# Three phases over edge tiles made into one software-pipelined loop, with the softmax state of a source node in one table

## The reference

```
# layer 3 (equivariant), after the per-edge messages were summed by node into agg
s_in, v_in = agg[..., 0:2], agg[..., 2:8]            # 64 channels, scalar and 3-vector
os1 = softplus(s_in @ w_f2o1_s / 8) - log 2 ; ov1 = v_in @ w_f2o1_v / 8
x3  = layernorm(x2 + concat(os1 @ w_f2o2_s, ov1 @ w_f2o2_v) / sqrt(128))
# layer 4 (attention over edges, 8 heads of 64, grouped by source node)
q, k, v = split(x3 @ W) ; aw = sum(q[src] * k[dst]) / 8    # one score per edge and head
e = exp(aw - segment_max(aw, src)[src])
out[n] = sum over edges of n (e * v[dst]) / sum(e)
x4 = layernorm(x3 + out)
```

## Time and profile before

| | us |
|---|---|
| three runs | 2404.39, 2409.9, 2411.34; median 2409.9 |
| the profiled execution's own time | 2407.08 |
| its span, first to last instruction | 2405.4 |

### The profile page before, as it was taken

How to read it: one execution, slowest core, us unless ns; L and a number is a source line. 1 busy time by engine, 2 the same in 40 slices (tenths; PEclk the granted TensorE clock), 3 DMA queues, 4 the chain that set the end, 5 groups by cost and what they waited for, 6 DMA issues and landing times. The chain is left out here.

```text
span 2405.4 us, 24073 instructions
## 1 busy us (share of the span) xinstructions
PE 1907.2 (79%) x5516; PEld 938.7 (39%) x5516; DVE 1583.2 (66%) x2672; ACT 1038.4 (43%) x1968; POOL 1007.9 (42%) x1095
## 2 busy tenths in 40 slices
PE   5999995999999999999999790055487699967800
PEld 2444442444444444444444340033255444423300
DVE  5464552577777777777776060799568679867854
ACT  2353442455555555555554230244278623313332
POOL 2211112466665666666656532456322012224334
PEclk9999998999999999999999895555568799979855
DMA  7632113444444444444443633433333222227743
GB/s 259 244 130 58 18 22 56 164 158 151 153 158 144 159 155 146 163 147 156 157 142 136 199 64 48 114 84 88 101 126 123 104 90 106 106 79 193 211 136 110
DMA packets 159454, 310.19 MB, mean 129 GB/s; under 512 B 31890, under 2 KB 45107, under 8 KB 159127
## 3 DMA queue, kind: packets, MB, share of 16 engines
q1 hardware_dynamic: 126278, 233.65, 28.0%
q0 software_dynamic: 29760, 71.21, 13.1%
q10 hardware_dynamic: 3344, 4.51, 0.6%
HBM read 169.54 MB, written 139.76 MB: 129 GB/s over the span
## 5 line engine op out<-in xcount | busy, mean ns | idle before, releaser
L659 PE MATMUL d_p_h<-w3a,d_xT 128*128 128x512 f32 x640 | 290.5, 597 | 25.4 <-DMA d_xT<-in_xT 25.4
L659 PE MATMUL d_p_o<-d_w,d_uT 128*128 128x512 f32 x640 | 289.9, 596 | 3.0 <-ACT d_uT L734 3.0
L659 PE MATMUL d_p_p<-d_wr,d_x1T 128*128 128x512 f32 x640 | 289.0, 595 | 0.0
L550 POOL TENSOR_SCALAR d_small<-d_mv 128x1 f32<-128x1 f32 x160 | 81.9, 512 | 303.5 <-DVE d_mv L785 153.7
L816 DVE TENSOR_TENSOR d_zz<-d_yg,d_xbeta 128x512 f32<-128x512 f32 x80 | 138.5, 1731 | 98.9 <-POOL d_yg L867 98.9
L659 PEld LDWEIGHTS d_p_h<-w3a,d_xT 128*128 128x128 f32 x640 | 122.8, 192 | 180.4 <-issue 180.4
L659 PEld LDWEIGHTS d_p_o<-d_w,d_uT 128*128 128x128 f32 x640 | 122.1, 191 | 156.6 <-issue 152.0
L727 ACT ACTIVATE d_yn<-d_y,d_small 128x512 f32<-128x512 f32 x80 | 65.1, 813 | 230.6 <-POOL d_small L555 230.6
L659 PEld LDWEIGHTS d_p_p<-d_wr,d_x1T 128*128 128x128 f32 x640 | 116.1, 191 | 115.9 <-issue 115.9
L282 PE MATMUL m_p_H<-m_xT,m_w 128*128 128x512 f32 x320 | 147.3, 615 | 4.8 <-ACT m_xT L323 4.8
L755 ACT ACTIVATE d_x<-d_zz,d_small 128x512 f32<-128x512 f32 x80 | 65.1, 814 | 178.4 <-POOL d_small L555 178.4
(11 more groups left out here) (252 smaller groups left out, 4239.2 us busy)
## 6 DMA issues: line engine op xcount, KB each, us to landing
sum<-d_zeros SPq DMA_DIRECT2D x80, 260.0 KB, 2.1
sum<-m_tile_sum SPq DMA_DIRECT2D x10, 2048.0 KB, 7.8
d_xT<-in_xT SPq DMA_DIRECT2D x80, 256.0 KB, 2.7
d_z<-sum SPq DMA_DIRECT2D x80, 256.0 KB, 2.9
d_x<-in_x SPq DMA_DIRECT2D x80, 256.0 KB, 3.4
x<-d_x SPq DMA_DIRECT2D x80, 256.0 KB, 2.0
p<-d_p SPq DMA_DIRECT2D x80, 256.0 KB, 2.0
pair_p<-p SPq DMA_DIRECT2D x40, 512.0 KB, 3.8
```

Source lines behind the costliest of these rows:

```text
L550: nc.gpsimd.tensor_scalar(tmp, var, factor, add, ALU.mult, ALU.add).then_inc(done, 1)
L659: last = nc.tensor.matmul(out[:, :], lhsT[:, c, :], w[:, c, :], start=(c == 0), stop=(c == KB - 1))
```

## The change

`equivariant_phase` and `scores_phase` become empty, and `values_phase` holds one block (names `f_`) with `STEPS = 25` steps. In step i, tile a = i is in the first product, b = i-1 in the second product and normalisation, c = i-2 in the queries and keys, d = i-3 in scores, tile maximum, values and weighing, e = i-4 in the merge with the node's state.

- The maximum is a running one. A new DRAM table `state` has 528 columns a node: for each head 64 weighted sums and the sum of weights, and at the end 8 maxima. For each tile POOL gathers the nodes' old state, DVE and ACT make the new maximum and the two factors exp(old max - new max) and exp(tile max - new max), DVE computes old * factor + tile sums * factor, and POOL scatters the result back (a plain write). `sum3`, `max3`, their gathers and the accumulating scatter are gone. The gather for tile t+1 waits until the scatter of t has landed.
- Scores are spread to all partitions by two transfers in place of PE and DVE work: SP writes the tile's 128x8 scores to DRAM, waits, and reads the row back broadcast to 128 partitions (512 KB). `cand` reads it with a stride of 8 elements.
- x3: the node's row is added by PE (identity times row, a 128x512 product) into the one `p_R`, whose vector part is written with a stride of 3 elements; ACT copies it out. DVE's two additions are gone, and w2s, w2v are scaled once.
- One buffer where there were two for `p_O`, `p_R`, `q`, `away` and `both`; queries and values share the PSUM bank `p_qv`. `outT` has 2 buffers of 2 units, where there were 3 of 4.
- Weights `wqk` (2 MB) and `wv` (1 MB) are loaded at the start, behind the first two pairs. Pairs are spread 3, 2, 2 and then 1, 2, 1, 2, ... over the 25 steps.
- `dense_phase` fills two tables in place of three; `attended_rows_phase` reads 528 columns and takes two reciprocals of 128x8 in place of one of 128x16.

The diff, cut to its core:

```diff
+def plain_plan(steps):
+    plan = [3, 2, 2] + [1 + i % 2 for i in range(steps - 3)]
...
-                sp.dma_start(rows(k.sum2, i), zeros[:, 0:8 * F]).then_inc(tables_set, 16)
-                sp.dma_start(rows(k.sum3, i), zeros[:, :]).then_inc(tables_set, 16)
-                sp.dma_start(rows(k.max3, i), lowest[:, :]).then_inc(tables_set, 16)
+                sp.dma_start(rows(k.sum2, i), empty[:, 0:8 * F]).then_inc(tables_set, 16)
+                sp.dma_start(rows(k.state, i), empty[:, :]).then_inc(tables_set, 16)
...
+        @block.sync
+            pair_load(nc, k, sp, 0)
+            pair_load(nc, k, sp, 1)
+            sp.dma_start(k.wqk, ...).then_inc(k.wqk_in, 16)
+            sp.dma_start(k.wv[:, :, :], ...).then_inc(k.wqk_in, 16)
+            for step in range(STEPS):
+                t = step - 3
+                if 0 <= t < T:
+                    sp.wait_ge(aw_done, t + 1)
+                    sp.dma_start(k.aw_rows[t, :]..., k.scores[:, t, :]).then_inc(aw_out, 16)
+                    sp.wait_ge(aw_out, 16 * (t + 1))
+                    if t:
+                        sp.wait_ge(cand_done, t)
+                    sp.dma_start(spread..., k.aw_rows[t:t + 1, :].to_broadcast([P, P * HEADS])).then_inc(spread_in, 16)
+                for _ in range(HERE[step - 1] if step else 0):
+                    if pair + 2 < PAIRS:
+                        pair_load(nc, k, sp, pair + 2)
+                    pair_store(nc, k, sp, pair)
+                    pair += 1
...
+        @block.gpsimd
+            for step in range(STEPS):
+                for u in (2 * step + AHEAD, 2 * step + AHEAD + 1):
+                    if u < 2 * T:
+                        gather_sums(u)        # waits until PE has turned unit u - 6
+                t = step - 4
+                if 0 <= t < T:
+                    scatter_state(t)          # waits for merged
+                    if t + 1 < T:
+                        gather_state(t + 1)   # waits until the scatter has landed
...
+        @block.tensor
+            for step in range(STEPS):         # (the "if tile in range" tests are cut)
+                second(b, 0)                  # waits ssp_done(b), y_done of the unit before
+                turn_x3(c, 0); turn_x3(c, 1)
+                second(b, 1)
+                turn_sums(a, 0)
+                queries(c)
+                first(a, 0); turn_sums(a, 1)
+                values(d)
+                first(a, 1)
+                keys(c)
+                tile_sums(d)                  # waits vw_done(d)
...
+        @block.scalar
+            for step in range(STEPS):
+                second_product_out(b, 0)      # y_done
+                x3_turned_out(c, 0); x3_turned_out(c, 1)
+                second_product_out(b, 1)
+                sums_turned_out(a, 0)
+                state_factors(e); away_from(d); query_out(c)
+                first_product_out(a, 0); sums_turned_out(a, 1)
+                x3_rows(b)
+                weights(d)                    # waits less_done(d)
+                first_product_out(a, 1); logarithms(a)
+                for _ in range(HERE[step]):
+                    pair_normalise(nc, k, act, pair)
+                    pair += 1
...
+        @block.vector
+            for step in range(STEPS):
+                scores(d); new_maximum(e)     # the latter waits old_in(e)
+                moments(b, 0); moments(b, 1)  # wait y_done
+                merge(e)                      # three 128x520 instructions
+                extra = HERE[step]
+                if extra:
+                    pair_leaky(nc, k, dve, pair)
+                    if extra == 1:
+                        pair_moments(nc, k, dve, pair)
+                        pair += 1
+                tile_maximum(d)               # cand, reduce, subtract: less_done
+                if extra > 1:
+                    pair_moments(nc, k, dve, pair)
+                    pair += 1
+                weigh_values(d)
+                softplus(a)                   # waits logarithms(a)
+                for _ in range(extra - 1):
+                    pair_leaky(nc, k, dve, pair)
+                    pair_moments(nc, k, dve, pair)
+                    pair += 1
```

More of the change, by code:

```diff
@@ new lines, in values_phase @@
+        cand = k.filters[:, :, :, :].rearrange("p t c f -> p (t c f)")[:, KB * 2 * D:KB * 2 * D + HEADS * P].rearrange(
+            "p (h e) -> p h e", h=HEADS)
+        away = sb("away", [P, P])
+        less, both = sb("less", [P, HEADS]), sb("both", [P, HEADS, HD + 1])
+        old = [sb(f"old{i}", [P, STATE + HEADS]) for i in range(2)]
+        new, part = sb("new", [P, STATE]), sb("part", [P, HEADS, HD + 1])
+        fall, factor = sb("fall", [P, 2, HEADS]), sb("factor", [P, 2, HEADS])
+        p_T = [ps(f"p_T{i}", [P, D]) for i in range(2)]
@@ new lines, in values_phase @@
+        q_done, q_out, k_done, prod_done, aw_done, aw_out, spread_in, away_done, cand_done, top_done, less_done = (
+            sem(n) for n in ("q_done", "q_out", "k_done", "prod", "aw", "aw_out", "spread_in", "away", "cand", "top",
+                             "less"))
+        weighed, v_done, vw_done, s_done, old_in, new_top, fall_done, factors, scaled, part_done, merged, gone = (
+            sem(n) for n in ("weighed", "v_done", "vw", "s_done", "old_in", "new_top", "fall", "factors", "scaled",
+                             "part", "merged", "gone"))
@@ L1444, in second @@
[L1444 to L1453, removed]
@@ new lines, in product, with queries @@
+            def product(out, xT, w, done):
+                for c in range(KB):
+                    last = nc.tensor.matmul(out[:, :], xT[:, c, :], w[:, c, :], start=(c == 0), stop=(c == KB - 1))
+                last.then_inc(done, 1)
+            def queries(t):
+                pe.wait_ge(turned_out, turn_number(t + 2, 0) + 1)
+                if t:
+                    pe.wait_ge(vw_done, t - 1)
+                    pe.wait_ge(q_out, t)
+                product(p_qv, srcT, k.wqk[:, :, 0:D], q_done)
@@ new lines, in weights, with state_factors @@
+            def weights(t):
+                act.wait_ge(less_done, t + 1)
+                if t:
+                    act.wait_ge(s_done, t)
+                nc.scalar.activation(both[:, :, HD], less[:, :], ACT.Exp).then_inc(weighed, 1)
+            def state_factors(t):
+                act.wait_ge(fall_done, t + 1)
+                if t:
+                    act.wait_ge(part_done, t)
+                nc.scalar.activation(factor[:, :, :], fall[:, :, :], ACT.Exp).then_inc(factors, 1)
+            nc.scalar.preload_act_table_set(ACT_SET)
@@ L1897, in _ @@
                 b, c = g % 2, g % BUFS
+                heads = [sums[c][:, s, 0:ATT].rearrange("p (h f) -> p h f", h=HEADS) for s in range(2)]
                 dve.wait_ge(sums_in[c], 32 * (g // BUFS + 1))
```

679 lines of the change are left out of this document (301 added, 378 removed).

## The result

The changed kernel is slower. Its median is 2433.4 us (2423.1 to 2434.6, five runs), that of the kernel before on the same chip 2404.4; the ratio is 1.0102, with a 95% interval of 1.0076 to 1.0129. The profiled execution's own time is 2433.4 us, 26 us above the 2407.1 of before.

What follows compares the result with a forecast made beforehand. DVE and PE, each 78% busy, were not full, so stream order decides. Steps end at 2303, the o phase starts at 2315 against 2313: +2, plus 10 of unseen costs, on 2407.1 gives 2419, forecast 2420; range 2375 to 2470.

Steps and rivals of the forecast that it cites:

- the side that had the higher chance: Whole kernel: slower, above 2417 us, was given 0.51, against 0.31 for faster and 0.18 for the same.
- DVE's work does not shrink: Fused loop: additions and diagonal go, the merge comes; 461 us of DVE work against 457 now.
- The two steps: Full loop: a two-pair step of 25.5 us and a one-pair step of 22.6, together 48.1 with 39.4 of DVE work.
- The stride at a tenth: Strided reads of cand and writes of p_R: a tenth more on cand, nothing on PE, 0.1 us a step.
- The third rival: Strided accesses at twice the price: cand 1.24 us more, PE's passes 0.7, in each of 20 steps; +39, 2458; 8%.
- Loads and state: Late pair loads behind the spread, 0.7 us in two steps, and late state scatter and gather, 0.4.
- The start: Steps 0 to 3: DVE starts at 1734, third pair lands at 1757, wanted at 1748; step 0 ends at 1764.
- The end: Steps from 20 on: 88.6 us in all, then 12 us from the last pair to the o phase's first gather.
- The first rival: Idle time in two steps falls from 8.7 to 4.4 us: -43 us, 2377; sign DVE over 88% busy; 27%.
- The second rival: Late normalisation holds y and state or pair transfers are late, at new_maximum or leaky: +32 us, 2450; 8%.
- The fourth: PE stays at the low clock: 34 us a step, +115 us, 2520; sign a clock under 0.7; 4%.

Runs made afterwards that it cites:

- kernels 3: The changed kernel with the stride of 8 elements moved from the addition of the candidates to the reduction that reads its result: 2433.2 us, ratio 1.0123.
- 12: The changed kernel with the spread table read contiguously, leaving out the reordering by head (maximum over the wrong scores): 2411.2 us, ratio 1.0038.
- kernel 5: The changed kernel with DVE adding the node rows itself again, without the identity product, ACT's copy and PE's stride: 2405.1 us, ratio 1.0002.
- kernel 1: The changed kernel with ACT normalising a step's last pair in the next step, behind the copies of y: 2410.5 us, ratio 1.0034.
- kernel 10: 7 plus the second half's product in the keys' PSUM bank and the logarithms ahead of the weights on ACT: 2373.6 us, ratio 0.9875.
- 13: kernel 10 with one maximum a node over all heads, so that the spread table is read contiguously: 2358.0 us, ratio 0.9809.
- kernel 11: 7 plus logarithms ahead of the weights on ACT and DVE adding the node rows itself: 2383.8 us, ratio 0.9916.
- 7: kernel 1 plus SP issuing a step's pair loads ahead of its wait for the scores: 2379.4 us, ratio 0.9891.

## Why the prediction held, and where not

Forecast 2420, measured 2433, in the range and on the side that had the higher chance. Against the kernel before it looks less good: +12 us were forecast and +26 measured on the profiled executions (+10 and +29 by medians), so the sign and the mechanism were right and the size was under half. On the own time of the profiled executions it was 2419 against 2433.4, 14 us short. By its terms:

- *DVE's work does not shrink*: right. 460.7 us busy for 461 forecast, though this hides an error: added up as I had added them, the durations are 477 us, 16 more, and the stride is 16. The busy time is lower because neighbouring records overlap a little. The merge, three times 0.70, and the softplus, 0.71, are as forecast.
- *The two steps*: the mechanism was right, each wait at its place. One-pair step: forecast waits 1.3 and 3.2, measured 1.51 and 3.62, and for the weights and logarithms some 2 forecast, 1.4 measured. Two-pair step: 0.7 and 1.5, measured 1.14 and 1.86, or 2.75 and 1.86 where PE began slowly. Per two steps the waits are 10.3 us (82.1 us in steps 4 to 19, in eighths) for 8.7 forecast, and all else 40.7 for 39.4. The means are 27.4 and 23.6 us for 25.5 and 22.6. The missing term is PE's clock after short stops: I gave the low level to the one stop of over 6 us, but four of the eight two-pair steps began slowly too, at 1.6 us each.
- *The stride at a tenth*: the step that failed in size. It costs 0.79 us on 1.22, 16 us in all for 2 forecast, shown by kernels 3 and 12. The third rival's 1.24 for DVE was nearer in its place than my 0.1 was, and the sign that I had set for it, `cand` over 2 us, came by a hair (2.008). For PE, taking nothing was right: its six strided passes take 0.83 us, like the contiguous ones before the change and in kernel 5. I had priced a stride of 32 bytes below the one of 12 bytes that the row showed, without a reason. The Trainium skill (SBUF — State Buffer, Door 1: The DMA port swizzle) asks for two accesses in each 16-byte line for full bandwidth; by that fp32 at 32 bytes has one, at 12 bytes one and a third. The measured two thirds and one fifth more agree with that order. The section of the Trainium skill also says that non-contiguous PSUM slows matmuls. The 0.83 us here disagree.
- *Loads and state*: 1.1 us in two steps were put down for them. In steps 4 to 19 DVE waited for neither, so 9 us of the sum had nothing behind them and hid as much of what was missing. But the loads were close: kernel 1 took 56 us of other waits away and 36 us of load waits appeared.
- *The start*: step 4 was forecast at 1829.5 and began at 1829.9, by errors that cancel. I had the third pair wait 9 us for its load; it waited 1.2, with 328 GB/s moved from 1730 to 1765, and DVE was through step 0 at 1759 in place of 1764. Step 2 gave 3 us of this back, a wait for the logarithms, and step 3 was 1.6 us longer than forecast.
- *The end*: last pair 94.3 us after step 20 began for 88.6 forecast, with 3.6 us for a load that I had not seen and a two-pair step 20 of 27.4 for 25; from there to the first gather of the o phase 7.3 us for 12:

```profile
2332.28 0.17 DVE L1161 TENSOR_SCALAR pair_neg<-pair_mv 128x2 f32<-128x2 f32 x1
...
2339.57 0.97 POOL L1875 DMA_INDIRECT o_sums<-state,index  x1 [25.09 <-PEq L1856]
```

The sum: steps 4 to 19 are 408 us in place of 385 + 10, +13; the last steps +6; the way to the o phase -5. That is the 14 us. In two of the steps 4 to 19 the waits are 1.6 us over the forecast and the stride 1.4, while the 1.1 for loads and state did not come. That the two ends nearly cancel, and that the 9 us for loads and state stood in for part of the stride, is luck; without those 9 us the forecast would have been 23 us short.

The first rival, a loop that packs better, was wrong for this kernel (DVE is busy 77% of steps 4 to 19, its sign was 88%) and is what the experiments made of it: two steps of 46.6 us in kernel 10 and 45.1 in kernel 13. The second rival's mechanism did not decide here (no wait for the state in steps 4 to 19), but its loads did in kernel 1. The fourth did not come: the clock is 0.84 in the stretch. That the stretch begins 3 us later than before needs no cause: in the thirteen profiled executions of the change and the experiments, which do the same work up to there, DVE's first instruction of the stretch (`f_w2s`) starts anywhere from 1726 to 1736. What stays open is the length of PE's slow stretch in a one-pair step. In steps 5, 9 and 15 it reached into the queries (4.2 to 4.5 us in place of 3.60), so that PE came too late to its sums to stand there for 1.3 us, and the next step began at full clock; in the others it ended earlier, and no run shows why.

## What to carry to other kernels

In a fused loop of in-order streams, write each engine's list by who waits for the item: work that nobody needs soon (here the normalisation of independent rows) goes behind all that another engine needs at once, and loads go ahead of any wait for this step's results. Do both: alone, the late normalisation made the full steps hardly shorter (51.0 to 50.6 us for two), since the loads took the place of the copy; with the loads it made them 47.5. An edit that takes work off the busiest engine is worth nothing if the engine that gets it has it in the wrong place of its list. And fix the orders before judging such an edit: DVE's own addition won 28 us in one order (kernel 5) and nothing in the other (kernel 11 beside 7 and 10).

## What the hardware showed that was not expected

- DVE, 1024 fp32 a partition: 1.22 us contiguous, 2.00 to 2.01 us with a stride of 32 bytes, alike for an addition of two inputs and a reduction of one.
- A 4 KB write from 128 partitions: the next transfer waited 1.0 us for it in pieces of 32 bytes, 10.8 us in pieces of 4 bytes.
- PE begins at 1.2 GHz even after a stop of 1.31 us, four passes and another stop of 0.69 us (2031 to 2033, where the granted clock of 2032.5 to 2037 is 0.62). In the changed kernel all five two-pair steps with a first stop of 1.3 us begin so (8, 12, 14, 18 and 20), and none of the four with 0.3 us or none. The length of that stop is not the whole rule: in kernel 5 steps 10, 16 and 18 begin at the high level after 1.4 to 1.8 us and 0.7.
